# Grams beside y, state products a slot ahead, and a reordered VectorE chunk in a fused SSD + mixture-of-experts layer

## The reference, cut to what matters

```
h    = rmsnorm(layernorm(x)) ; z, x', B, C, dt_raw = h @ w_in_proj
x'   = silu(causal_conv(x'))      dt = softplus(dt_raw @ w_dt + b_dt), mean per head
lcs  = cumsum(dt * A)             M = exp(lcs_i - lcs_j), masked to j <= i
G    = C B^T                      y = (M * G) x' + exp(lcs) C state
state= exp(lcs_end) * state + sum_l M[end, l] x'_l B_l
x    = x + x_norm + rmsnorm((y + D x') * silu(z)) @ w_out
x    = x + layernorm(x) + shared experts / 2 + top-2 routed experts   (relu MLPs, 128 -> 512 -> 128)
```

## Time and profile before

| | us |
|---|---|
| median of 3 runs (575.64 to 581.18) | 577.71 |
| the profiled execution, its own time | 576.64 |
| its span, first to last instruction | 574.9 |
| PE busy | 548.7 (95%) |
| DVE busy | 437.6 (76%) |
| ACT busy | 356.2 (62%) |
| POOL busy | 172.6 (30%) |
| one body, from one lcs to the next (280.2 to 346.4 us) | 66.2, of which PE 65.17 |

### The profile page before, as it was taken

How to read it: one execution, slowest core, us unless ns; L and a number is a source line. 1 busy time by engine, 2 the same in 40 slices (tenths; PEclk the granted TensorE clock), 3 DMA queues, 4 the chain that set the end, 5 groups by cost and what they waited for, 6 DMA issues and landing times.

```text
span 574.9 us, 11864 instructions
## 1 busy us (share of the span) xinstructions
PE 548.7 (95%) x4016; PEld 429.8 (75%) x4016; DVE 437.6 (76%) x1037; ACT 356.2 (62%) x767; POOL 172.6 (30%) x232
## 2 busy tenths in 40 slices
PE   8886999999999999999999999999999999999996
PEld 7665767877777777877787777777778787777774
DVE  4878767887789785888688786987768787676654
ACT  3894488637675477636795477745787376852442
POOL 2073504521163202631046201622036210542011
PEclk9999999999999999999999999999999999999999
DMA  6650006300550006600272004700064003510120
GB/s 204 183 152 2 0 33 190 84 1 2 147 173 3 1 6 175 143 1 0 81 173 65 0 0 155 164 0 0 15 198 106 0 1 105 157 44 1 38 59 21
DMA packets 37354, 41.43 MB, mean 72 GB/s; under 512 B 3482, under 2 KB 27716, under 8 KB 37316
## 3 DMA queue, kind: packets, MB, share of 16 engines
q1 hardware_dynamic: 36724, 40.80, 25.9%
q10 hardware_dynamic: 592, 0.15, 0.1%
HBM read 37.79 MB, written 3.15 MB: 71 GB/s over the span
## 4 chain that ended last, share of the span: by engine, by line
PE 48%; DVE 19%; issue 11%; ACT 9%; DMA 5%; POOL 5%; SPq 1%; DVEq 0%; ACTq 0%; POOLq 0%
PE bank L424 7%; PE bank L426 5%; PE bank L425 5%; PE bank L535 4%; PE bank L642 4%; PE bank L644 4%; PE bank L643 4%; DVE act_l L1268 4%; DVE cv L1121 4%; DMA grow<-lc_rows 3%; ACT act_h L874 3%; PE bank L547 2%; PE bank L563 2%; PE bank L435 2%; ACT L967 2%
## 5 line engine op out<-in xcount | busy, mean ns | idle before, releaser
L1268 DVE SCALAR_TENSOR_TENSOR act_l<-bank,act_h 128x512 fp32r<-128x512 f32 x192 | 131.3, 686 | 69.8 <-ACT act_h L874 68.6
L874 ACT ACTIVATE act_h<-bank 128x512 fp32r<-128x512 f32 x192 | 114.1, 594 | 81.9 <-PE bank L426 78.0
L424 PE MATMUL bank<-fTl,w1h 128*128 128x512 f32 x192 | 86.9, 452 | 3.0 <-DVE fTl L1219 2.3
L1492 POOL TENSOR_TENSOR late<-late 128x512 f32<-128x512 f32 x31 | 39.8, 1285 | 163.3 <-DVE late L1276 163.3
L894 ACT ACTIVATE seg<-seg,lneg 128x128 f32<-128x128 f32 x256 | 81.2, 391 | 2.8 <-DMA seg<-lc_rows 2.8
L642 PE MATMUL bank<-act_l,w2h 128*128 128x512 f32 x192 | 77.5, 404 | 1.6 <-DVE act_l L1268 1.5
L425 PE MATMUL bank<-fTh,w1l 128*128 128x512 f32 x192 | 75.7, 394 | 0.0
L644 PE MATMUL bank<-act_h,w2h 128*128 128x512 f32 x192 | 75.6, 394 | 0.0
L426 PE MATMUL bank<-fTh,w1h 128*128 128x512 f32 x192 | 75.6, 394 | 0.0
L643 PE MATMUL bank<-act_h,w2l 128*128 128x512 f32 x192 | 75.2, 392 | 0.0
L1479 POOL TENSOR_TENSOR xw<-xs,seg 128x128 f32<-128x128 f32 x48 | 19.9, 414 | 157.3 <-ACT seg L894 82.8
(11 more groups left out here) (176 smaller groups left out, 1063.6 us busy)
## 6 DMA issues: line engine op xcount, KB each, us to landing
seg<-lc_rows SPq DMA_DIRECT2D x32, 512.0 KB, 4.5
late<-gk_rows SPq DMA_DIRECT2D x8, 1024.0 KB, 9.3
grow<-lc_rows SPq DMA_DIRECT2D x48, 128.0 KB, 5.4
x_in<-L_attn_hidden_dram SPq DMA_DIRECT2D x8, 256.0 KB, 3.7
out_dram<-late SPq DMA_DIRECT2D x8, 256.0 KB, 2.5
late<-L_ffn_sw_dram SPq DMA_DIRECT2D x2, 512.0 KB, 7.2
late<-L_ffn_rw_dram SPq DMA_DIRECT2D x1, 1024.0 KB, 7.7
CT<-L_attn_w_in_proj_dram SPq DMA_DIRECT2D x1, 512.0 KB, 5.3
```

The costliest lines, as they stand in the source:

```text
L424: mm(dst, stat_h, mov_l, start=True, stop=False)
L874: nc.scalar.activation(act_h[:, b % RING, :], HID[b % 2][:], ACT.Relu).then_inc(act_h_ready, 1)
L1268: v_.scalar_tensor_tensor(act_l[:, r, :], HID[b % 2][:], 0.0, f(act_h[:, r, :]), ALU.max, ALU.subtract)\
```

## The change: what it does

1. `lcs`: `dta` gets 32 columns per chunk, so the four 32-column matmuls on array quarters become one full 128-column matmul. `kept` likewise: the four quarter matmuls of `g_transposes` become one transpose.
2. PE order: `gram(c + 1)` moves from step 1 of chunk c + 1 to the head of `y_product(c)`; the state products move from `y_product(c)` to step 1 of chunk c, a slot ahead.
3. DVE order: `mg` of chunks 1 and 2 moves to step 0 (first half at the slot's head, second half behind `act_low`), of chunk 3 to the head of slot 21; `next_state(c)` moves to step 1 behind `act_low`; `norm1(s + 1)` moves from slot 15 to the end of slot 16, `norm1_apply(s + 1)` from slot 18 to the end of slot 19; `store(older)` moves behind `act_low`; the second tap of the convolution's second block moves from slot 2 to slot 3.
4. ACT order: `b_copy(3)` moves ahead of slot 6's `relu`, both `xs_copy` behind it.
5. SP order: the store of `older` is issued behind `segments(s, 0)`.

`opening()` gets items 1 and 2; its DVE order stays.

```diff
@@ SP body
-                if older is not None:
-                    sp_eng.wait_ge(out_ready, nth(older, 1, 1))
-                    sp_eng.dma_start(out_dram[older], out_t).then_inc(out_stored, 16)
...
                     segments(s, 0)
+                if older is not None:
+                    sp_eng.wait_ge(out_ready, nth(older, 1, 1))
+                    sp_eng.dma_start(out_dram[older], out_t).then_inc(out_stored, 16)
+                if s is not None:
                     segments(s, 1)
@@ PE lcs
-                mm(sums[:, 0:32], upto[:], dta[:, 0:32], start=True, stop=True)
-                for c in range(NCH):
-                    ins = mm(sums[32 * c:32 * c + 32, P:2 * P], dta[:, c * NH:c * NH + 32], upto[:], start=True, stop=True)
-                ins.then_inc(lcs_psum, 1)
+                mm(sums[:, 0:32], upto[:], dta[:, :, 0:NH], start=True, stop=True)
+                mm(sums[:, P:2 * P], dta[:].rearrange("p c q -> p (c q)"), upto[:], start=True, stop=True).then_inc(lcs_psum, 1)
@@ PE state_product, y_product
+            def state_product(s, c):
                 if c > 0:
                     pe.wait_ge(state_step, nth(s, 8, (2, 5, 8)[c - 1]))
+                pe.wait_ge(btok_ready, nth(s, 3, c + 1))
+                pe.wait_ge(xw_ready, nth(s, 6, 2 * c + 2))
+                for n in range(NP):
+                    ins = mm(MAIN[1][:, n * 64:(n + 1) * 64], btok[:, at(n)], xw[:, n, :, :].rearrange("p t d -> p (t d)"),
+                             start=True, stop=True)
+                ins.then_inc(s_psum, 1)
+
+            def y_product(s, c):
+
+                if c == NCH - 1:
+                    pe.wait_ge(state_step, nth(s, 8, 8))
                 if c < NCH - 1:
-                    (the same state products)
+                    gram(s, c + 1, None)
@@ PE g_transposes
-                for c in range(NCH):
-                    ins = mm(MAIN[2][32 * c:32 * c + 32, 0:P], kept[:, c * NE:c * NE + 32], ident[:], start=True, stop=True)
-                ins.then_inc(gT_psum, 1)
+                nc.tensor.transpose(MAIN[2][:, 0:P], kept[:].rearrange("p c q -> p (c q)"), ident[:]).then_inc(gT_psum, 1)
@@ PE scan_part
-                    if step == 1:
+                    if step == 1 and c == 0:
                         gram(s, c, prev)
+                    if step == 1 and c < NCH - 1:
+                        state_product(s, c)
@@ ACT body
+                    if s is not None and i == 6:
+                        b_copy(s, 3)
                     if new := block_at(i, prev, older):
                         relu(*new)
-                    if s is not None and i in (5, 6):
-                        b_copy(s, i - 3)
-                        xs_copy(s, i - 5)
+                    if s is not None and i == 5:
+                        b_copy(s, 2)
+                    if s is not None and i == 6:
+                        xs_copy(s, 0)
+                        xs_copy(s, 1)
@@ DVE scan_part, body
-                if i == 15 and not last:
-                    norm1(s + 1)
-                if i == 18 and not last:
-                    norm1_apply(s + 1)
...
+                        if i in (15, 18, 21):
+                            masked_gram(s, i // 3 - 4, 0)
+                        if i == 21:
+                            masked_gram(s, 3, 1)
...
                     if (new := block_at(i, prev, older)) and not (i == 0 and prev is not None):
                         act_low(*new)
+                    if older is not None and i == (7 if s is not None or prev is None else 9):
+                        store(older)
+                    if s is not None and i in (15, 18):
+                        masked_gram(s, i // 3 - 4, 1)
+                    if s is not None and i in (13, 16, 19):
+                        next_state(s, i // 3 - 4)
+                    if s is not None and i == 16 and not is_seq(s, n_seq - 1):
+                        norm1(s + 1)
+                    if s is not None and i == 19 and not is_seq(s, n_seq - 1):
+                        norm1_apply(s + 1)
...
-                            conv(s, 1, (0, 1))
+                            conv(s, 1, (0,))
                         if i == 3:
-                            conv(s, 1, (2, 3))
+                            conv(s, 1, (1, 2, 3))
```

More of the change, by code:

```diff
@@ L180, in build @@
         rank = sb("rank", [P, NCH * NE])
-        kept = sb("kept", [P, (NCH - 1) * NE + 32])
+        kept = sb("kept", [P, NCH, 32])
         gT = sb("gT", [P, P])
@@ L704, in scan_part @@
                         b_tokens(s, c, prev, older)
-                    if step == 1:
+                    if step == 1 and c == 0:
                         gram(s, c, prev)
-                        if c == NCH - 1 and not is_seq(s, n_seq - 1):
-                            proj(s + 1, 0)
+                    if step == 1 and c < NCH - 1:
+                        state_product(s, c)
+                    if step == 1 and c == NCH - 1 and not is_seq(s, n_seq - 1):
+                        proj(s + 1, 0)
                     if step == 2:
@@ L785, in opening @@
                         b_tokens(0, c, None, None)
-                    gram(0, c, None)
+                    if c == 0:
+                        gram(0, c, None)
                     if c < 2:
@@ new lines, in masked_gram @@
+            def masked_gram(s, c, hf):
+                dve.wait_ge(g_psum, nth(s, 8, 2 * c + hf + 1))
+                dve.wait_ge(decay_masked, nth(s, 8, 2 * c + hf + 1))
+                if hf == 0 and (v := nth(s, 4, c)) is not None:
+                    dve.wait_ge(y_psum, v)
+                v_.tensor_tensor(mg[:, hf], MAIN[2 + hf][:].rearrange("p (n l) -> p n l", n=NP), decay(c)[:, hf], ALU.mult)\
+                    .then_inc(mg_ready, 1)
+            def attend(s, c, step):
+                if step == 1 and (c == 0 or is_seq(s, 0)):
+                    masked_gram(s, c, 0)
+                    masked_gram(s, c, 1)
+                if step == 2:
+                    if c < NCH - 1 and is_seq(s, 0):
+                        next_state(s, c)
@@ L1182, in attend, with next_state @@
                     v_.tensor_tensor(yT[:, :, at(c)], yT[:, :, at(c)], szT[:, :, at(c)], ALU.mult).then_inc(yz_ready, 1)
+            def next_state(s, c):
+                first = (0, 2, 5)[c]
+                if c > 0:
+                    dve.wait_ge(grow_ready, nth(s, 3, c))
+                    v_.tensor_tensor(state_m[:], state[:, (c - 1) % 2], grow[:, c % 2, :, P - 1:P].to_broadcast([P, NP, 2 * HD]),
+                                     ALU.mult).then_inc(state_step, 1)
+                    dve.wait_ge(state_step, nth(s, 8, first + 1))
+                    first += 1
+                dve.wait_ge(s_psum, nth(s, 3, c + 1))
+                own = MAIN[1][:, 0:256].rearrange("p (n d) -> p n d", n=NP)
+                for t in range(2):
+                    q, d = slice(64 * t, 64 * t + 64), slice(HD * t, HD * t + HD)
+                    if c == 0:
+                        v_.tensor_copy(state[q, c % 2, :, d], own[q, :, d]).then_inc(state_step, 1)
+                    else:
+                        v_.tensor_tensor(state[q, c % 2, :, d], own[q, :, d], state_m[q, :, d], ALU.add).then_inc(state_step, 1)
+                dve.wait_ge(state_step, nth(s, 8, first + 2))
             def mean_square(s):
@@ L1323, in body @@
                             gT_copy(prev)
-                    if older is not None and i == (7 if s is not None or prev is None else 9):
-                        store(older)
                     if older is not None and i == 3 + LAG:
@@ L1398, in opening @@
                     scan_part(0, i)
+                    if i == 15:
+                        norm1(1)
+                    if i == 18:
+                        norm1_apply(1)
                     if i == NBLK - 4:
```

44 lines of the change are left out of this document (7 added, 37 removed).

## The result

| | before | after |
|---|---|---|
| median (range) | 577.6 (575.64 to 581.18) | 599.1 (598.12 to 600.01) |
| ratio | 1 | 1.0376, 95% 1.0343 to 1.0409 |
| span of the profiled execution | 574.9 | 597.3 |
| body: mean of the five from the lcs of body 2 to that of body 7 | 66.45 | 69.61 |
| the six bodies from the lcs of body 1 to that of body 7 | 398.0 | 416.2 |

The forecast was 578.2 with a range up to 586.0. The kernel became 21.5 us slower. Of the 22.4 us between the two spans, 18.2 lie in the six bodies from lcs to lcs, 2.9 in the opening and 1.4 behind the last lcs. So the loss repeats in every body (2.0 to 4.0 each).

What follows compares the result with a forecast made beforehand. PE's own instruction stream was the bound. Savings of 1.8 us per body against 0.4 + 0.9 + 0.7 + 0.25 gave +2.7 over bodies 1 to 6; with -1.4 (body 7) and -0.8 (opening), +0.5: 578.2, range 572 to 584, with rivals 568 to 586.

Steps and rivals of the forecast that it cites:

- Part 1: lcs and kept on the full array: PE's stream gains 0.34 and 0.45 us per body.
- Part 3: BT 3 copied earlier on ACT: proj 11's wait goes, gain 0.66 us per body; the moved tap costed at nothing.
- Part 2: Grams beside y in the chunks: fewer array switches on PE, gain 0.34 us per body.
- Part 5: norm1 a slot on: state products of chunk 2 in slot 19 wait for xw(2), loss 0.9 us per body.
- Part 6: norm1_apply a slot on: hn transposes in slot 20 wait for hn, loss 0.7 us, bounds 0.4 to 1.0.
- Part 7: Slots 20 to 23: DVE enters later with more to do, loss 0.25 us per body, bounds 0 and 0.8.
- Part 4: Slots 13 and 14: gram(1) waits for mg of chunk 0, loss 0.4 us per body, bounds 0 and 1.4.
- the first gate: Slot 14: PE's wait for mg of chunk 0, fed by DMA rows and ACT; loss 0.4 us per body.
- Rival (d): Full-array lcs and transpose no cheaper than the side-by-side quarters: about +3 us, so 581; chance 0.04.
- The disputed switch: Slots 14, 17 and 20, 64-row halves to 32-column quarters: 0.10 us taken, bounds 0 and 0.10.
- Rival (b): Growth rows or softplus hold mg(0) by DVE's and DMA's clock: +1.0 us in 7 bodies, 585.2; chance 0.13.
- rival (c): Waits for xw, hn and slots 20 to 23 at their upper ends: +7.5 us, 585.7; chance 0.08.

Runs made afterwards that it cites:

- e14: Kernel before with single matmuls for lcs and kept, ACT's new order, store behind act_low, SP's growth rows ahead of segments 1 and store: 567.0 us, ratio 0.9812.
- e10: Changed kernel with norm1 back in slot 15, norm1_apply at the end of slot 18, SP's growth rows and segments 1 ahead of the store: 570.3 us.
- e13: Changed kernel with only SP's order altered, growth rows and segments 1 ahead of the store; norm1 and norm1_apply as changed: 590.1 us, ratio 1.0204.
- e17: e14 with the convolution's tap 1 of the second block in slot 3 behind fT_low: 567.2 us, ratio 0.985.
- e5: Kernel before with only the single matmuls for lcs and kept: 577.2 us, ratio 0.9979.
- e8: e5 with ACT's new order of b_copy(3) and the xs copies in slots 5 and 6: 577.7 us, ratio 0.9994.
- e12: e10 with norm1_apply moved on to the end of slot 19, norm1 staying in slot 15: 582.3 us, ratio 1.0079.

## Why the prediction was wrong, step by step

The sum's terms against what the runs showed, over the whole kernel. The measured chain is before, e14, e10, e13, after, each the difference of two medians, and beside it the six bodies from lcs to lcs in the traces:

| step | forecast | measured | six bodies |
|---|---|---|---|
| Parts 1 and 3 with the opening's lcs | -10.5 | -10.6, once the rows are first (e14) | -9.7 |
| Part 2 and the rest of the opening | -2.9 | +3.3 (e14 to e10) | +1.8 |
| Parts 5, 6, 7, the norm | +11.1 | +19.8 (e10 to e13) | +18.6 |
| Part 4, the first gate | +2.8 | +9.0 (e13 to after) | +7.5 |
| sum | +0.5 | +21.5 | +18.2 |

The first row's agreement is partly luck: e14 also loses about 1.7 us of mg waits that the kernel before had and that no Part counted.

**Part 1: right, 0.1 too large in all.** Forecast 0.34 and 0.45. lcs with its neighbours is 0.26 shorter (0.93 to 0.67), kept with its neighbours 0.45 (1.02 to 0.57), and 0.10 is lost again in slot 9, where a matmul reaches its start 0.02 late and the next stands 0.33 off. Rival (d) falls.

**Part 2: the number right, its effect nil.** The disputed switch adds 0, not 0.10. Against that, state products that stand alone make the next matmul's step 0.31 or 0.32 (371.87 to 372.19) instead of 0.23, three times a body, which the sum left out. The gain up to the hn transposes is 0.47. In the bodies nothing of it arrives (64.99 in e10 and in e17): the two waits in slot 22 take it back. In the opening the sign was wrong: roughly +2, not -0.8.

**Part 3: right in PE's stream, cover included.** The wait at proj 11 is gone, proj 10's has grown by the tap (0.34 from its neighbour's start without it in e14, 0.67 with it in e17). That the tap brings nothing was forecast, and e17 bears it out.

**Part 4: the step that failed first.** The step reads "SP's store moved behind the first segments pulls seg 0 forward, but not the growth rows". The growth rows did not stay where they were: they left 0.9 later after lcs, since SP now waits for a DVE store that itself stands behind act_low. I counted that delay in a half sentence ("segments(1) and the growth rows wait behind it") and gave it no us. growth(1) waits 1.45 in the body shown, gram(1) 1.46 in place of 0.4; over bodies 1 to 7 gram(1)'s excess is 0, 0.3, 1.5, 0.9, 1.5, 1.1 and 1.7, together 7.0 for a forecast of 2.8. Rival (b) described exactly this, with its mark, and priced it at +1.0 per body; e13 to after makes it (9.0 - 2.8) / 7 = 0.9, the waits alone 0.6. Its mechanism was right, its price nearly so, and its chance of 0.13 too low. e5 and e8 show that the gate was shut before the change. Part 4 had it waiting in three to four bodies, by the listed waits of the earlier trace rows; read as distances, L563 stood 0.06 behind mg in six of seven. And the read that came late there was mostly seg 0 (2.8 us of ACT's waits, against 0.8 at growth(1)), while Part 4 looked at the growth rows alone.

**Part 5: the size nearly right, the place half missed.** Forecast 0.9 at xw. Measured 0.51 there and 0.51 at second(12), which waits for the routed term behind norm1: 1.0, and 1.2 with the longer step behind each; e12 to e13 makes it 1.35 per body. The routed term is what the forecast did not name. POOL's chain (rsqrt1 1.65, xw, select, xw) came as counted.

**Part 6: mis-sized, 2.0 against 0.7, the largest miss.** The cover was counted right: from second (390.50) PE would have reached the first transpose at 393.40, 1.59 ahead of 394.99, and the last, which the forecast counts to, at 393.73, 2.03 ahead of 395.76. e10 to e12 makes it 1.77 per body, above the bound of 1.0. The chain was not. From act_low's start (391.33) to hn's end (395.71) it took 4.4, of which state_m 0.92 for 0.42 and hn 1.92 for 1.1 to 1.7. The sentence that failed is "The late CTe(2) and add_term(0) end at about the time at which hn begins". They did; but CTe(3) begins then, since it waits for y(2) just as hn's transposes do. So hn and CTe(3) meet in all six bodies, in e12 and e13 too. The stretched instruction of hn, which ends 0.08 behind CTe(3), and state_m at 0.92 are what the loss adds to the rows. The Trainium skill ("SBUF — State Buffer", two separate sides) has VectorE and GpSimd lock one shared port pair for a whole instruction. By that rule I had given 1.0 for this part. The trace agrees with it, with the 1.15 that ends with CTe(3) (1.31 in e12) and the 0.92, and no run here shows the ports themselves.

**Part 7: 0.45 against 0.25** (second(16) 0.28, proj(s+1, 0) 0.17), inside its bounds, but not the norm's doing: e10 has the same two waits. Besides, behind the stall for hn the clock fell in two of the bodies. Windows of the changed kernel in such a body and in one without it (columns: PE busy, PEld, DVE, ACT, POOL, granted clock, DMA share, GB/s):

```profile
325.50:329.20 3.70, 3.70 (x11) 2.91 (x10) 2.73 (x6) 1.34 (x3) 0.00 (x0) 0.54 0.00 0
396.00:400.00 4.00, 4.00 (x18) 2.94 (x18) 3.29 (x8) 2.19 (x5) 0.00 (x0) 1.00 0.00 0
```

0.54 is near the 1.2 GHz level, and matmuls stood 0.43 apart instead of 0.23. By the clock alone this costs 3.70 x 0.46 = 1.7 us each, but the two bodies are only 0.5 and 0.7 longer than their neighbours (70.15 and 70.31 against 69.65), since PE then waits less elsewhere. e13 has the same stall for hn and no such fall in a body. Its bodies are 3.12 longer than e10's, 1.77 by norm1_apply and 1.35 by norm1: this is rival (c)'s upper end, reached by Parts 5 and 6 without Part 7.

**The rivals as a set.** (b) and (c) came true together. The range stopped at either of them alone: both added are 578.2 + 7.0 + 7.5 = 592.7. The 6.4 us from there to 599.1 are, by the table, Part 2 and the opening, which lost 3.3 where 2.9 had been booked as a gain. (b) and (c) feed on the same thing, a PE that runs ahead of chains timed by DVE, POOL and DMA. They were treated as alternatives, and they add.

What stays open: what the store and segments 1 each contribute at the first gate, which only body 1 separates; how much of the opening's loss is the grams and how much the clock; and why the clock fell in two bodies with the stall and not in others.

## What to carry to other kernels

A saving on the bounding engine pays only up to the next point where it meets a chain with another clock. Before you sum savings, look at how far behind its releaser the engine starts at that point, in every body and not only in the listed waits: here PE started 0.06 us behind mg in six of seven bodies, and this said that what is saved ahead of it would be lost. Reordering SP's queue, so that the reads of the chain stand ahead of a store that waits for another engine, turned savings that had moved nothing (577.7) into 567.0. And a total of waits for one tile can mix places: only 0.8 of the 8.1 us for growth rows stood at this gate. When a step is moved later, look not only at how late it ends but at what it now runs beside. And bounds of gates that one cause feeds are to be added for the range, not put side by side.

## What the runs showed of the hardware

- Four VectorE tensor_scalar of 128x128 took 1.11 with GpSimd idle, and 1.92 and 2.08 beside its 1.26 us tensor_tensor. One of the four took all of the difference and ended 0.08 or 0.09 us behind the GpSimd instruction, in each body with hn of the changed kernel, e12 and e13. A tensor_tensor of 128x256 took 0.42, and 0.92 beside a select.
- A gram on 64-row halves stood 1.09 us ahead of what followed, whether full-array matmul or 32-column quarters, while the switches between the full array and quarters cost 0.10 and 0.11.
- Behind a matmul that had waited, even by 0.02 us (363.56), the next 128x512 matmul stood 0.33 off instead of 0.23.
- A stall of 1.5 us for hn was followed in two of the bodies by 3.7 us at a granted clock of 0.54, and in another (396 to 400 us) by none.
